# A gated delta rule layer with one head woven into the next: key work and key products in earlier slots, the inverse's products in later ones, and the second set of diagonal blocks fetched from ScalarE's queue

## The reference

```python
qkvz = x @ W_qkvz                       # per key head: q, k (128 each), v, z (256 each)
qkv = silu(causal_conv1d(qkv, conv_weight))          # 4 taps
q, k = l2norm(q) * Dk ** -0.5, l2norm(k)
g = cumsum(g within a chunk)
decay_mask = tril(exp(clip(g_i - g_j, -30, 30)))
attn = -(k_beta @ k.T * decay_mask), strictly lower
for i in 1 .. 63: attn[i] += attn[i] @ attn          # (I + A)^-1 row by row
attn += I
value_corrected = attn @ v_beta
k_cumdecay = attn @ (k_beta * exp(g))
for c in chunks:                                     # 8, one behind the other
    v_prime = v_c - k_cumdecay_c @ state
    out = (q_c @ state) * exp(g_c) + tril(q_c k_c.T * decay_mask) @ v_prime
    state = state * exp(g_last) + (k_c * exp(g_last - g)).T @ v_prime
out = rmsnorm(out * silu(z), norm_weight) @ W_out
```

## Time and profile before

| | |
|---|---|
| median of 3 runs | 5451.85 us |
| profiled execution | 5436.97 us, span 5434.8 us |
| mean granted clock of TensorE | 0.963 |
| TensorE, products busy | 4886.2 us (90%) |
| VectorE busy | 3511.8 us (65%) |
| ScalarE busy | 3036.7 us (56%) |
| GpSimd busy | 1063.5 us (20%) |

### The profile page before, as it was taken

One profiled execution on the slowest core, in us unless ns is written; L12 is line 12 of the kernel. 1 busy time (PEld: TensorE's weight loads), 2 busy tenths in 40 slices (PEclk: granted clock), 3 DMA queues, 4 the chain that ended last, 5 costly groups with the idle time before them and its releaser, 6 DMA issues.

```text
span 5434.8 us, 140777 instructions
## 1 busy us (share of the span) xinstructions
PE 4886.2 (90%) x52272; PEld 3409.1 (63%) x52272; DVE 3511.8 (65%) x6423; ACT 3036.7 (56%) x7909; POOL 1063.5 (20%) x1064
## 2 busy tenths in 40 slices
PE   3777799999999889999999899999999999999998
PEld 1555566666666666666666666666666666666666
DVE  6444566666666666666666666666666666666665
ACT  2222465656656555655656556565666566566565
POOL 0000122222222122122222122222222222222222
PEclk7888899999999999999999999999999999999999
DMA  1111322222222222222222212222222222222221
GB/s 48 29 29 29 84 58 59 56 62 44 58 59 64 67 52 59 55 61 44 60 59 71 68 44 58 57 58 53 52 58 71 67 44 60 59 55 60 54 51 39
DMA packets 686346, 300.55 MB, mean 55 GB/s; under 512 B 599153, under 2 KB 642289, under 8 KB 675441
## 3 DMA queue, kind: packets, MB, share of 16 engines
q1 hardware_dynamic: 685680, 291.60, 22.4%
HBM read 212.76 MB, written 66.07 MB: 51 GB/s over the span
## 4 chain that ended last, share of the span: by engine, by line
PE 56%; issue 15%; DVE 10%; ACT 8%; SPq 5%; DMA 3%; POOL 2%; DVEq 0%; POOLq 0%; ACTq 0%
PE pj L617 9%; PE dsb L754 7%; PE ms L675 6%; SPq L427 4%; PE pj L612 4%; ACT arena L889 4%; PE pot L683 4%; PE pot L712 3%; DVE cy L1171 3%; PE pod L695 3%; PE dsb L726 3%; PE ms L644 2%; PE ms L630 2%; PE pod L738 2%; PE ms L659 2%
## 5 line engine op out<-in xcount | busy, mean ns | idle before, releaser
L617 PE MATMUL pj<-xnT,wt 128*128 128x512 f32 x2048 | 1005.5, 619 | 86.6 <-ACT arena L889 56.6
L1171 DVE SCALAR_TENSOR_TENSOR cy<-xpad,cw,cy 128x1024 f32<-128x1024 f32 x768 | 1063.3, 1391 | 15.7 <-ACT cy L909 5.5
L1419 POOL TENSOR_TENSOR rout<-rin,expo 128x2 f32<-128x2 f32 x512 | 365.1, 713 | 2769.9 <-DVE rin L1307 2769.9
L617 PEld LDWEIGHTS pj<-xnT,wt 128*128 128x128 f32 x2048 | 354.6, 190 | 490.4 <-issue 347.2
L754 PE MATMUL dsb<-wo,yT 128*128 128x256 f32 x2048 | 588.3, 411 | 13.7 <-issue 12.5
L1413 POOL TENSOR_TENSOR sdec<-st,gel 128x512 f32<-128x512 f32 x384 | 402.2, 1048 | 992.9 <-DVE st L1296 861.3
L908 ACT ACTIVATE xpad<-pj 128x512 f32<-128x512 f32 x512 | 302.5, 591 | 470.4 <-PE pj L617 469.5
L967 ACT ACTIVATE yT<-dsb 128x256 f32<-128x256 f32 x512 | 196.4, 384 | 595.3 <-PE dsb L745 594.3
L612 PE MATMUL pj<-wt,xnT 128*128 128x256 f32 x2048 | 510.1, 392 | 0.0
L1286 DVE SCALAR_TENSOR_TENSOR rr<-pot,nge,arena 128x128 f32<-128x128 f32 x896 | 271.1, 344 | 336.8 <-PE pot L683 336.8
L754 PEld LDWEIGHTS dsb<-wo,yT 128*128 128x128 f32 x2048 | 357.0, 194 | 126.2 <-issue 95.8
(11 more groups left out here) (163 smaller groups left out, 8367.8 us busy)
## 6 DMA issues: line engine op xcount, KB each, us to landing
qge<-ge_rows SPq DMA_DIRECT2D x64, 1024.0 KB, 7.3
wt<-in_L_attn_W_qkvz SPq DMA_DIRECT2D x64, 768.0 KB, 4.4
gb<-g_rows SPq DMA_DIRECT2D x128, 256.0 KB, 4.3
a_d<-at SPq DMA_DIRECT2D x64, 512.0 KB, 2.7
wo<-in_L_attn_W_out SPq DMA_DIRECT2D x64, 256.0 KB, 2.8
x_d<-xpair SPq DMA_DIRECT2D x128, 128.0 KB, 1.7
ap_<-a_d SPq DMA_DIRECT2D x512, 16.0 KB, 1.8
dd<-x_d SPq DMA_DIRECT2D x512, 16.0 KB, 1.8
```

Of the source, the lines that this page charges most:

```text
L617: last = mm(pj[n % 2][:, :], wt[:, k, col:col + DH], batch(xnT, k, i), start=(k == 0), stop=(k == KD - 1))
L1171: stt(y, x[:, :, tap:tap + SEQ], cw[:, kind, tap:tap + 1], y, ALU.mult, ALU.add).then_inc(S["conv"], 1)
L1419: tt(rout[:, :], rin[:, :], expo[:, 0, 0:GRP], ALU.pow).then_inc(S["routs"], 1)
```

## The change

Seven things are moved, and no arithmetic changes. Numbers are slots.

- The ring's order: the second z fill goes ahead of the second v0 fill. The fills' slots on TensorE become 0, 1, 2, 4, 5, 7, 8, 10, 11, 11, 13, 14, 16, 17 and four times 23, where the last two stand behind the last product round. ScalarE's copies stand in the same slots, but for the first z copy (4), and the silu and squares of the key stand ahead of the copy of q.
- The key's sums of squares and key products: 7 to 5. Coefficients on VectorE: 8 to 5, and the scaled decay and first matrix to 6.
- The inversion of the blocks: rows 1 to 4 in 11, rows 5 to 7 in 12, the join from 14 cut over 14 and 15.
- The off-diagonal products: 17 to 19; the three product rounds: 19, 20, 22 to 20, 22, 23.
- The transfers into ee are started by ScalarE in 17, when the second store has landed, and no longer by SyncE behind those into dd.
- The weights wt are fetched when the last z fill has been computed, without waiting for the convolution; only cw waits for it.
- The query's decay products on VectorE move from 21 to the next core's step 0, ahead of its first slot.

```diff
@@ the ring of PSUM fills
-        ring = [("k", 0), ("k", 1), ("z", 0), ("q", 0), ("q", 1), ("v0", 0), ("v0", 1), ("kt", 0), ("kt", 1),
-                ("v1", 0), ("v1", 1), ("z", 1), ("z", 2), ("z", 3), ("vt", 0), ("vt", 1), ("vt", 2), ("vt", 3)]
+        ring = [("k", 0), ("k", 1), ("z", 0), ("q", 0), ("q", 1), ("v0", 0), ("z", 1), ("v0", 1), ("kt", 0), ("kt", 1),
+                ("v1", 0), ("v1", 1), ("z", 2), ("z", 3), ("vt", 0), ("vt", 1), ("vt", 2), ("vt", 3)]
...
+        def blocks_back(eng, n, dst, done):
+
+            for r in range(GRP * NBLK):
+                eng.dma_start(dst[r * BLK:(r + 1) * BLK, :, (r % NBLK) * BLK:(r % NBLK + 1) * BLK],
+                              x_d[r * U:(r + 1) * U, n].rearrange("u j i -> j u i")).then_inc(done, 16)
@@ SyncE, load_weights
                 after(sp, "proj", g - 1, last_projected)
                 apart(sp)
-                before(sp, "conv", g)
-                apart(sp)
                 sp.dma_start(wt[:, :, :], w_qkvz.rearrange("(k p) n -> p k n", k=KD)[
                     :, :, bass.ds(hk * HEADCOLS, HEADCOLS)]).then_inc(d_w, 16)
+                before(sp, "conv", g)
+                apart(sp)
@@ SyncE, relayout_back
-                for n, (dst, done) in enumerate(((dd, d_dd), (ee, d_ee))):
-                    loaded(sp, (d_x0, d_x1)[n], g, 1)
-                    apart(sp)
-                    for r in range(GRP * NBLK):
-                        sp.dma_start(dst[r * BLK:(r + 1) * BLK, :, (r % NBLK) * BLK:(r % NBLK + 1) * BLK],
-                                     x_d[r * U:(r + 1) * U, n].rearrange("u j i -> j u i")).then_inc(done, 16)
+                loaded(sp, d_x0, g, 1)
+                apart(sp)
+                blocks_back(sp, 0, dd, d_dd)
@@ TensorE, fill_ring
                 if n < 2:
-                    before(pe, "pcopy", g)
+                    after(pe, "pcopy", g - 1, RING - 1 + n)
@@ TensorE, front_piece
-                if s == 7:
+                slots = (0, 1, 2, 4, 5, 7, 8, 10, 11, 11, 13, 14, 16, 17, 23, 23, 23, 23)
+                for n in range(RING - 2):
+                    if s == slots[n]:
+                        fill_ring(g, p, n, hk == 0)
+                if s == 5:
                     square_sums(g, 0)
                     chunk_squares(g, p, 0)
...
-                for n, at_s in enumerate((1, 2, 4, 5, 5, 8, 10, 13, 13, 14, 14, 16, 17, 20, 22, 22, 23, 23)):
-                    if s == at_s:
-                        fill_ring(g, p, n, hk == 0)
                 for n in range(2):
-                    if s == 17:
+                    if s == 19:
                         off_products(g, p, n)
-                for n, at_s in enumerate((19, 19, 20, 20, 22, 22)):
+                for n, at_s in enumerate((20, 20, 22, 22, 23, 23)):
                     if s == at_s:
                         fixpoint(g, p, n // 2, n % 2)
+                for n in range(RING - 2, RING):
+                    if s == slots[n]:
+                        fill_ring(g, p, n, hk == 0)
@@ ScalarE, front_piece (the silu of both v, and both negations, move as well)
+                slots = (0, 1, 4, 4, 5, 7, 8, 10, 11, 11, 13, 14, 16, 17, 23, 23, 23, 23)
...
+                if s == 17:
+                    loaded(act, d_x1, g, 1)
+                    apart(act)
+                    before(act, "yadd", g)
+                    apart(act)
+                    blocks_back(nc.scalar, 1, ee, d_ee)
-                if s == 18:
+                if s == 20:
                     silu(g, p, 2)
-                if s == 20:
+                if s == 22:
                     silu(g, p, 3)
...
-                        empty_ring(g, p, n)
                         if n == 3:
                             silu(g, p, 0)
                             squares(g, p, 0)
+                        empty_ring(g, p, n)
@@ VectorE: join_halves is cut in two, join_left (three instructions) and join_right (the last reduction)
-                if s == 8:
+                if s == 5:
                     coefficients(g, p)
+                if s == 6:
                     scale_decay(g)
                     decayed_squares(g, p, 0)
                 if s == 11:
+                    invert_rows(g, 1, 5)
+                if s == 12:
                     query_eps(g, p)
-                if s == 12:
-                    invert_rows(g, 1, 5)
-                if s == 13:
-                    invert_rows(g, 5, 7)
+                    invert_rows(g, 5, 8)
                 if s == 14:
-                    invert_rows(g, 7, 8)
-                    join_halves(g)
+                    join_left(g)
                 if s == 15:
+                    join_right(g)
                     turn_inverse(g)
                     decayed_squares(g, p, 1)
-                for n, at_s in enumerate((3, 3, 5, 6, 9, 9, 11, 11, 17, 17, 18, 18)):
+                for n, at_s in enumerate((2, 3, 3, 8, 8, 9, 17, 17, 18, 18, 20, 21)):
                     if s == at_s:
                         convolve(g, n // 3, n % 3 + 1)
-                for n, at_s in enumerate((19, 19, 20, 20, 22, 22)):
+                for n, at_s in enumerate((20, 20, 22, 22, 23, 23)):
                     if s == at_s:
                         add_round(g, p, n // 2, n % 2)
-                if s == 21:
-                    for h in range(GRP):
-                        decayed_queries(g, p, h)
@@ VectorE, core
+                    if c == 0:
+                        for h in range(GRP):
+                            decayed_queries(g, p, h)
                     fill(3 * c)
```

More of the change, by code:

```diff
@@ L344, in load_weights @@
                 apart(sp)
+                sp.dma_start(wt[:, :, :], w_qkvz.rearrange("(k p) n -> p k n", k=KD)[
+                    :, :, bass.ds(hk * HEADCOLS, HEADCOLS)]).then_inc(d_w, 16)
                 before(sp, "conv", g)
                 apart(sp)
-                sp.dma_start(wt[:, :, :], w_qkvz.rearrange("(k p) n -> p k n", k=KD)[
-                    :, :, bass.ds(hk * HEADCOLS, HEADCOLS)]).then_inc(d_w, 16)
                 kq = conv_w.rearrange("c a t -> c (a t)")
@@ L978, in front_piece @@
                     output_weights(g, p)
-                if s == 18:
+                for n in range(2):
+                    if s == 19:
+                        negated(g, n)
+                if s == 17:
[5 more added lines that the diff above has]
+                if s == 20:
                     silu(g, p, 2)
-                if s == 20:
+                if s == 22:
                     silu(g, p, 3)
-                for n in range(2):
-                    if s == 17:
-                        negated(g, n)
-                for n, at_s in enumerate((1, 2, 4, 5, 5, 8, 10, 13, 13, 14, 14, 16, 17, 20, 22, 22, 23, 23)):
-                    if s == at_s:
-                        empty_ring(g, p, n)
+                for n in range(RING):
+                    if s == slots[n]:
                         if n == 3:
@@ L1249, in invert_rows, with join_left @@
                                       ).then_inc(S["sub"], 1)
-            def join_halves(g):
-                w = BLK // 2
+            w = BLK // 2
+            def join_left(g):
                 pr = cells(prod[:, :], 0, (w * w, w), (w, w), (1, w))
@@ L1262, in join_halves, with join_right @@
                    ALU.mult).then_inc(S["sub"], 1)
+            def join_right(g):
+                pr = cells(prod[:, :], 0, (w * w, w), (w, w), (1, w))
                 after(dve, "sub", g, 16)
```

## The result

The kernel after takes 5178.31 us, the median of 4 runs (5176.92 to 5183.14), against 5451.53 (5444.49 to 5458.73) for the kernel before in the same comparison: 0.9500 of its time, 95% interval 0.9484 to 0.9517. The profiled execution took 5178.37 (span 5176.3).

The account below looks back on a forecast made before the run. TensorE's in-order list was the bound, with 4.64 us of stops a head. Terms left 2.8; 1.84 × 63 = 116, less 11, gave 105 off 5437: 5332 profiled, 5340 predicted as median, range 5235 to 5465.

Parts of the forecast that it names:

- rival 1: TensorE's clock gives back more as stops shorten and low-clock stretches get rarer: 70 us more, 5270; chance 0.15.
- (b): Slot 11, second key transpose: TensorE waits 0.9 us a head for the PSUM bank ScalarE empties; key-copy stop goes.
- (d): Off-diagonal products at slot 19: earlier inverse and later products shrink the stop on dd from 1.3 to about 0.1 us.
- (a): First key's squares, products moved from slot 7 to 5: TensorE waits 0.3 us a head for ScalarE's squares.
- (c): Solves waiting for VectorE's residuals, inverse spread out: wait 0.7 us, plus 0.3 each at slots 8 and 17.
- (e): ScalarE's slot 17: eight ee issues hold it 3.6 to 5 us, priced at nothing because slot 19 covers it.
- (f): Head's end, last value fills in slot 23: 0.3 stop goes, cost 0.1, weights 1.5 us spare; quarter starts cost 11 us.
- rival 2: SP's and ScalarE's queues share an issue limit, so dd ends 3.8 us later: 5580; chance 0.13.
- rival 3: ScalarE's hold for ee issues delays the tail's work; 1 us late in each head is 63 us: 5400; chance 0.14.
- rival 4: No change: weights or tail slip by 3 us and k0 holds the first solve: 5450; chance 0.08.

Follow-up runs that it names:

- b_sq12: Kernel before, with only the second sums of squares and query products moved from slot 11 to 12: 5363.85 us, ratio 0.9834.
- b_off19: Kernel before, with only the off-diagonal products moved from slot 17 to 19 and the product rounds and sums later: 5309.33 us, ratio 0.9733.
- a_stop_sq: Kernel after, with ScalarE's v0 copies and one added unused square ahead of the second squares, making them late: 5239.04 us, ratio 0.9602.
- a_off17: Kernel after, with off-diagonal products back in slot 17 and product rounds in 19, 20 and 22: 5458.15 us, ratio 1.0007.
- a_ee_sp: Kernel after, with the eight transfers into ee back in SyncE's queue behind those into dd: 5234.26 us, ratio 0.9600.
- a_join_twice: Kernel after, with one more unused 512-element product on VectorE in slot 14, ahead of residual 5: 5242.55 us, ratio 0.9619.
- a_join13: Kernel after, with v0 copies ahead of the second squares, the join's first product and reduction in slot 13, its rest in 14: 5095.57 us, ratio 0.9337.

## Why the prediction was wrong

Its sum gave 5332 for the profiled execution. 58 us more of idle time went than it had (163 against 105), and 95 us of clock came back that it priced at nothing: 5332 − 58 − 95 = 5179, and 5178.4 was measured.

**The step that failed is the clock.** I saw the 1.7 us of full speed lost in one stretch and wrote that some heads have it and some not; the sum then rebuilt "only the waits", and the clock became rival 1, 70 us at a chance of 0.15. The loss was 1.5 us a head in the mean (94.9 / 64), and b_sq12 shows that 58.6 us of it hung on the very stop that part (b) removed. b_off19, the move of part (d) alone, gave back 41.7, and the two together 79.0. My argument against it, that stops of 0.9 and 0.7 remain, fails by their length: after has stops of 0.4 to 0.5 in these places and 3 slow heads. What stops of 0.9 and 0.7 there would have done no run shows; one of 1.09 ahead of the squares lowered the clock 23 times in 65 (a_stop_sq). Rival 1's mechanism was the right one, and it comes on top of the forecast and not beside it: its own 5270 is above the result, since the idle terms were too small as well.

**The terms of the sum**, in us a head:

| part | predicted | measured |
|---|---|---|
| (a) first squares, L633 | 0.3 | 12.5 / 64 = 0.20 |
| (b) second key transpose, L605 | 0.9 | 30.4 / 64 = 0.48 |
| (c) residuals, L715 | 0.7 + 0.3 + 0.3 | 34.1 / 64 = 0.53 |
| (d) dd, L662 | 0.1 | 22.4 / 64 = 0.35 |
| (e) ee, L678 | 0 | 11.6 / 64 = 0.18 |
| sum | 2.6 | 1.73 |

(a) was right. (b) had its place right; ScalarE's bank was free 4.75 us after the solve's start (I had 5.1), and TensorE came at 4.4 (4.2). (c) in slot 14: VectorE from state update to the end of the residual took 5.06 us, 5.1 predicted, with the join's product at 1.76 against 1.02, the +0.7 I had estimated; TensorE came at 5.5, and the wait is 0.46. The 0.3 at slots 8 and 17 are not there: at slot 17 the timeline shows none. (d) was counted right from the solve (dd's first issue at +2.9, 3.2 predicted), but the sentence ahead of it, that the inverse comes some 4 us ahead of its old place, is wrong for the solve it is measured by: dd's issue is 1.8 later, and a_off17 shows what that costs without slot 19. I had counted this move as worth 1.2 us a head; it is the move on which the rest stands. (e) ScalarE stood for 3.8 us of issues, 4.29 of idle in all, and it cost nothing visible: L678 starts without a wait where the window shows it, and the move is worth 56 us in this kernel. (f) was too dear: the tokens land in 5.3 us, not 7.8, and the three further quarters lose 19.0 − 14.7 = 4.3 us, not 8. Its sum for the weights was also wrong: 5.7 less 1.4 and 4.1 leaves 0.2 us and not 1.5; it did no harm, as the cw transfers land in 1.9 us now.

**The rivals.** The shared limit of the queues (rival 2) is refuted by 448 and 470 ns. By the rule that I had set beside it (the Trainium skill, DMA: Bandwidth & Descriptors, Issuing engines are not separate DMA queues), only the sequencer's time is saved; the trace agrees, and here that time, 3.8 us for eight issues, was what counted (a_ee_sp). The tail (rival 3) did not slip: solve 7 and L610 have no wait of size. The weights of rival 4 are waited for in no ordinary head: the wait on cw comes three times, once in each later quarter, 6.2 us in all, 9.5 before. The periods are 71.6 us, against the 73.8 that I had named.

## What to carry to other kernels

Where one engine is over 90% busy and its clock can fall, price a stop twice: its length, and the excess of the groups right behind it, which the timeline of before shows head by head. Compare the busy time of equal instructions over the whole stretch with that at full clock (here 94.9 us) before the sum is made. And ask of each piece of a cut and moved chain how late it is against the engine that waits for it, not against the clock on the wall: one move can be what makes all others affordable, and moves of a set need not add up.

## What the runs showed of the hardware

- Behind a stop of 1.38 us ahead of one-column products, with 64-column ones after them, the granted clock fell in most heads (49 of 65 stops in before) and the groups behind took up to 1.74 times their time (1.13 for 0.65). Stops of 1.25 to 1.5 ahead of 64-column products alone left it at full (20 of 20 in a_ee_sp), and so did one of 1.44 ahead of a solve and a wide projection (63 of 63 in a_join_twice). One of 2.42 there lowered it (1.99 became 3.11), and so did stops of 2.3 us and more ahead of 64-column products (60 of 64 in a_off17). The Trainium skill (TensorE: Matmul & The Clock Gate, Part 1) says that the gate goes by how busy the engine has been; the runs agree and add that the place of the stop matters as well as its length. In b_off19 the same stop on the squares left 29 slow heads instead of 51 once another stop had gone; why is open.
- VectorE beside GpSimd: the two query products took 4.05 us in their new place, beside GpSimd's work, and 2.35 in the old; the join's product 1.76 against 1.02, and in a_join13 its second product 1.84 against 1.09. No row of the waits names the query products.
